# Retention in spans of 64 tokens, two side by side, with a middle state and another order of the steps

## The reference, cut to what matters

```python
def make_decay(length):                       # N_HEADS = 16, HEAD_DIM = 16
    gamma = 1.0 - 2.0 ** (-5.0 - jnp.arange(N_HEADS))
    diff = n - m
    return jnp.where(diff >= 0, gamma ** diff, 0.0)
...
for i in range(2):
    p = layer_norm(x) @ proj_w[i] + proj_b[i]
    q, k, v, xo = jnp.split(p, 4, axis=-1)    # each into 16 heads of 16
    scores = jnp.einsum('bhld,bhmd->bhlm', q, k) * D[None]
    ret = jnp.einsum('bhlm,bhmd->bhld', scores, v)
    ret = ret * jax.nn.silu(xo)
    x = x + ret @ reto_w[i] + reto_b[i]
    h = gelu(layer_norm(x) @ ffn1_w[i] + ffn1_b[i]) @ ffn2_w[i] + ffn2_b[i]
    x = x + h
```

## Time and profile before

| | |
|---|---|
| three runs | 1582.61, 1589.01, 1590.4 us |
| median | 1589.01 us |
| the profiled execution: span from first to last instruction | 1579.5 us |
| the profiled execution: its own time | not given apart from its span |
| TensorE matmul busy | 1351.4 us, 86% of the span |
| DVE busy | 1011.0 us, 64% |
| ACT, POOL busy | 614.6 us, 571.9 us |

### The profile page before, as it was taken

The page is one execution under the profiler, slowest core; times in us unless marked ns, Lnnn a source line. Parts: engine busy times, 40 slices in busy tenths (PEclk is TensorE's granted clock), DMA queues, the critical chain, the costliest instruction groups (busy, mean ns, idle before and its releaser), DMA issues.

```text
span 1579.5 us, 30698 instructions
## 1 busy us (share of the span) xinstructions
PE 1351.4 (86%) x11824; PEld 1104.9 (70%) x11824; DVE 1011.0 (64%) x2391; ACT 614.6 (39%) x1034; POOL 571.9 (36%) x460
## 2 busy tenths in 40 slices
PE   6871968876999999999998999999999676496885
PEld 3461968644788888888886888888887446496753
DVE  5661536658977877777768778797787453253623
ACT  5630635422333433343344334424455262263410
POOL 0726033352342323224424443364343704304252
PEclk9975979989999999999999999999999788698998
DMA  9963559650000000000010000000002463355542
GB/s 326 372 213 122 174 175 321 206 190 23 28 2 2 1 2 1 1 2 32 8 58 1 1 15 2 15 15 14 2 28 89 167 229 131 124 181 171 156 150 90
DMA packets 113867, 151.63 MB, mean 96 GB/s; under 512 B 12224, under 2 KB 96192, under 8 KB 113728
## 3 DMA queue, kind: packets, MB, share of 16 engines
q1 hardware_dynamic: 99328, 114.02, 21.8%
q0 software_dynamic: 12288, 33.57, 6.6%
q10 hardware_dynamic: 2112, 2.10, 0.4%
HBM read 78.21 MB, written 71.43 MB: 95 GB/s over the span
## 4 chain that ended last, share of the span: by engine, by line
PE 53%; DVE 16%; another core or an unknown queue 8%; issue 2%; ACT 2%; POOL 0%; DVEq 0%; ACTq 0%
PE l_w_ps L83 8%; PE l_w_ps L85 7%; PE l_w_ps L84 7%; DVE l_probs L2221 4%; PE l_banks L2505 3%; PE l_rm_ps L2537 2%; PE l_banks L83 2%; PE l_banks L84 2%; PE l_banks L85 2%; DVE l_f_lo L2252 2%; PE l_rm_ps L2530 2%; DVE l_full L2174 1%; PE b_gu_ps L83 1%; PE b_t_ps L1284 1%
## 5 line engine op out<-in xcount | busy, mean ns | idle before, releaser
L2221 DVE TENSOR_TENSOR l_probs<-l_banks,l_past 128x512 f32<-128x512 f32 x256 | 160.1, 684 | 29.8 <-PE l_banks L2505 29.7
L1964 ACT ACTIVATE l_act_f<-l_w_ps,l_ffn_b 128x512 f32<-128x512 f32 x120 | 82.7, 690 | 169.0 <-PE l_w_ps L85 163.9
L83 PE MATMUL l_w_ps<-l_w_hi,l_f_hi 128*128 128x256 f32 x496 | 143.6, 290 | 2.6 <-DVE l_f_lo L2252 2.4
L84 PE MATMUL l_w_ps<-l_w_lo,l_f_hi 128*128 128x256 f32 x496 | 139.6, 281 | 0.0
L85 PE MATMUL l_w_ps<-l_w_hi,l_f_lo 128*128 128x256 f32 x496 | 139.5, 281 | 0.0
L2059 POOL TENSOR_TENSOR l_g_lo<-l_q,l_g_hi 128x1024 fp32r<-128x1024 f32 x16 | 39.1, 2447 | 266.9 <-ACT l_g_hi L1955 266.9
L813 POOL DMA_INDIRECT b_picked<-rows,b_pos_i x64 | 61.1, 955 | 137.4 <-DMA rows<-b_yb 88.5
L83 PE MATMUL l_w_ps<-l_b_hi,l_w_hi 128*128 128x512 f32 x240 | 102.2, 426 | 0.3 <-ACT l_f_hi L1965 0.3
L83 PEld LDWEIGHTS l_w_ps<-l_w_hi,l_f_hi 128*128 128x128 f32 x496 | 93.3, 188 | 8.8 <-issue 8.7
L2252 DVE TENSOR_TENSOR l_f_lo<-l_act_f,l_f_hi 128x512 fp32r<-128x512 f32 x128 | 85.9, 703 | 18.5 <-ACT l_f_hi L1965 18.4
L2046 POOL TENSOR_TENSOR l_q_wide<-l_q,l_pair_mask 128x1024 f32<-128x1024 f32 x32 | 60.1, 1899 | 103.7 <-DVE l_q L2189 100.0
(11 more groups left out here) (432 smaller groups left out, 4053.0 us busy)
## 6 DMA issues: line engine op xcount, KB each, us to landing
rows<-a_zeros SPq DMA_DIRECT2D x14, 1024.0 KB, 10.7
a_xb<-rows SPq DMA_DIRECT2D x46, 256.0 KB
rows<-a_yb SPq DMA_DIRECT2D x46, 256.0 KB
b_xb<-rows SPq DMA_DIRECT2D x46, 256.0 KB
rows<-b_yb SPq DMA_DIRECT2D x46, 256.0 KB
a_w_in<-in_moe_w SPq DMA_DIRECT2D x15, 384.0 KB, 10.2
low_dram<-a_w_lo SPq DMA_DIRECT2D x15, 384.0 KB
b_w_lo<-low_dram SPq DMA_DIRECT2D x15, 384.0 KB
```

The costliest lines, as they stand in the source:

```text
L83: tensor.matmul(out, w_hi, x_hi, start=start, stop=False)
L84: tensor.matmul(out, w_hi, x_lo, start=False, stop=False)
L1964: nc.scalar.activation(act_f[:, f, :], hidden_ps(b, f), ACT.Gelu, bias=ffn1_b[:, b.layer, f:f + 1]).then_inc(act_done, 1)
L2221: dve.tensor_tensor(probs[c % 2][:, r * w:(r + 1) * w].rearrange("p (h n) -> p h n", n=P), banks[:, r, :].rearrange("p (h n) -> p h n", n= ...
```

## The change

- A chunk of 128 tokens is now two spans of 64 (`SPAN`, `SPANS`), done side by side in two halves of the array. Decays, mask and `own_head` are those of 64 tokens.
- `scores`: 16 matmuls instead of 8, on 32 rows by 64 columns, eight tiles, 128 moving columns instead of 256. A bank `banks[:, r]` holds 256 columns of scores instead of 512.
- values (in `retain`): 32 matmuls instead of 16, on 64 rows by 32 columns, eight tiles, 64 moving columns instead of 128.
- `outer`: 16 matmuls instead of 8, on 64 rows by 32 columns, eight tiles, 128 moving columns as before.
- state (in `retain`): 16 matmuls instead of 8, on 128 rows by 32 columns, four tiles, 64 moving columns; the first span takes `state`, the second the new `middle` (the state between the two spans). They now stand behind the values.
- `masked`: 128x256 instead of 128x512, in two pairs with `copy_keys` between them. `update_state`: one product of 128x512 instead of 128x256, then two instructions for `middle` and two for `state`. The last chunk of a batch now has `turn_keys`, `outer` and an update of `middle` too.
- Result, keys and outer products share the two banks of `rm_ps`. So `turn_keys` waits for `gated_done` instead of `state_done`, and `retain` waits until the outer products are read (`state_step`).
- Order on TensorE: scores(c+1), keys, one feed, outer, remaining feeds, values, state. `FEEDS` is now ((0,), (1, 2), (3, 4), (5, 6, 7)).

The core of the diff:

```diff
-        FEEDS = ((0,), (1, 2), (3, 4, 5), (6, 7))
+        FEEDS = ((0,), (1, 2), (3, 4), (5, 6, 7))
...
-        ret_ps, m_ps = rm_ps[:, 0, :], rm_ps[:, 1, :]
+        ret_ps, keys_ps, m_ps = rm_ps[:, :, 0:P], rm_ps[:, :, P:2 * P], rm_ps[:, :, 2 * P:]
...
-                        dve.tensor_tensor(probs[c % 2][:, r * w:(r + 1) * w].rearrange("p (h n) -> p h n", n=P),
-                                          banks[:, r, :].rearrange("p (h n) -> p h n", n=P),
-                                          past[:, :].unsqueeze(1).broadcast_to([P, 4, P]), ALU.mult).then_inc(probs_done, 1)
+                        dve.tensor_tensor(probs[c % 2][:, r * w:(r + 1) * w].rearrange("p (h n) -> p h n", n=SPAN),
+                                          banks[:, r, 0:w].rearrange("p (h n) -> p h n", n=SPAN),
+                                          past[:, 0:SPAN].unsqueeze(1).broadcast_to([P, 4, SPAN]), ALU.mult).then_inc(probs_done, 1)
...
+                        dve.tensor_tensor(fresh[:, 0:n, :, :], products[:, 0:n, :, :], own, ALU.mult).then_inc(state_step, 1)
+                        dve.wait_ge(state_step, before + 1)
+                        for g in range(KD):
+                            last = dve.scalar_tensor_tensor(middle[:, g, :], state[:, (k - 1) % 2, g, :], state_decay[:, g:g + 1],
+                                                            fresh[:, 0, g, :], ALU.mult, ALU.add)
+                        last.then_inc(state_step, 1)
...
+                        for h in range(SPANS):
+                            keys, own = slice(h * SPAN, (h + 1) * SPAN), span(c, h)
+                            for r in range(NQ):
...
+                                last = pe.matmul(banks[keys, r, g * PH * SPAN:(g + 1) * PH * SPAN], kT[rows, g, own], q_wide[rows, g, :, own],
+                                                 start=True, stop=True)
...
+                                last = pe.matmul(m_ps[quad, h, g * P:(g + 1) * P], ks[keys, w],
+                                                 v_wide[keys, c, g * NQ:(g + 1) * NQ, 0::PH, :], start=True, stop=True)
...
+                    pe.wait_ge(state_step, STATE_STEPS * cc - a.batch + (2 if k == 0 else 1))
+                    for g in range(KD):
+                        for i in range(PH):
+                            for h in range(SPANS):
...
+                                    pe.matmul(ret_ps[r * QUAD:(r + 1) * QUAD, h, g * SPAN:(g + 1) * SPAN],
+                                              v_wide[keys, c, g * NQ + r, i:i + PH, :].rearrange("p i x -> p (i x)"),
+                                              probs[c % 2][keys, head * SPAN:(head + 1) * SPAN],
...
+                                w = middle[:, g, quad] if h else state[:, (k - 1) % 2, g, quad]
+                                last = pe.matmul(ret_ps[quad, h, g * SPAN:(g + 1) * SPAN], w, q[:, g, span(c, h)], start=False, stop=(g == KD - 1))
```

More of the change, by code:

```diff
@@ L74 @@
 PH = QUAD // HD
+SPAN = P // 2
+SPANS = P // SPAN
 WEIGHT_PIECES = 2 * KD + 3
@@ new lines, in update_state @@
+                def update_state(a, cc, k):
+                    dve.wait_ge(st_done, cc + 1)
+                    products = m_ps.rearrange("p h (g n) -> p h g n", g=KD)
+                    n = SPANS if k < UPDATES else 1
+                    own = own_head[:, :, :].unsqueeze(1).broadcast_to([P, n, KD, P])
+                    before = STATE_STEPS * cc - a.batch
+                    if k == 0:
+                        dve.tensor_tensor(fresh[:, 1, :, :], products[:, 1, :, :], own_head[:, :, :], ALU.mult).then_inc(state_step, 1)
+                        dve.tensor_tensor(middle[:, :, :], products[:, 0, :, :], own_head[:, :, :], ALU.mult).then_inc(state_step, 1)
+                    else:
+                        dve.tensor_tensor(fresh[:, 0:n, :, :], products[:, 0:n, :, :], own, ALU.mult).then_inc(state_step, 1)
[4 more added lines that the diff above has]
+                        last.then_inc(state_step, 1)
+                    if k == UPDATES:
@@ L2242, in update_state @@
                         return
-                    dve.tensor_tensor(fresh[:, :, :], part, own_head[:, :, :], ALU.mult).then_inc(fresh_done, 1)
-                    dve.wait_ge(fresh_done, (UPDATES - 1) * batch + k)
+                    dve.wait_ge(state_step, before + 2)
                     for g in range(KD):
-                        last = dve.scalar_tensor_tensor(state[:, k % 2, g, :], state[:, (k - 1) % 2, g, :], state_decay[:, g:g + 1],
-                                                        fresh[:, g, :], ALU.mult, ALU.add)
@@ L2248, in update_state @@
-                    last.then_inc(state_done, 1)
+                        last = dve.scalar_tensor_tensor(state[:, k % 2, g, :], middle[:, g, :], state_decay[:, g:g + 1],
+                                                        fresh[:, 1, g, :], ALU.mult, ALU.add)
+                    last.then_inc(state_step, 1)
                 def low_feed(b, f):
@@ L2500, in scores @@
                             pe.wait_ge(k_done, KD * (a.n + 1))
-                        for r in range(NQ):
-                            if g == 0 and c > 0:
-                                pe.wait_ge(probs_done, NQ * (cc - 1) + r + 1)
-                            rows = slice(r * QUAD, (r + 1) * QUAD)
-                            last = pe.matmul(banks[:, r, g * PH * P:(g + 1) * PH * P], kT[rows, g, t], q_wide[rows, g, :, t],
-                                             start=True, stop=True)
-                            if g == KD - 1:
-                                last.then_inc(scores_done, 1)
```

164 lines of the change are left out of this document (86 added, 78 removed).

## The result

The changed kernel is slower. Its median is 1601.7 us (four runs, 1595.96 to 1608.64) against 1585.91 us for the kernel before beside it (four runs, 1582.61 to 1590.4). The ratio is given as 1.0158, 95% interval 1.0117 to 1.020; these two medians alone give 1.0100. So the loss is 16 to 24 us. It lies above my range, and the mechanism that did it is not among my rivals. The profiled execution has a span of 1606.9 us, 27 more than before. It took 1608.6 us, 1.7 more than its span; so the 9.5 us between the span and the median of the kernel before are not time outside the span, as I wrote, but mostly the distance of its profiled run from the median.

What follows compares the result with a forecast made beforehand. TensorE was taken to bound the retention steps. Per step 3.44 us less, minus 1.64, 0.33 and 0.11, nets 1.36; over 16 steps 21.8 us, so 1589.0 becomes 1567 us, range 1553 to 1594.

Steps and rivals of the forecast that it cites:

- two more instructions of 0.31 follow (+0.61): VectorE's state update: two added instructions cost 0.61 us per chunk, beside +0.27 for the wider product.
- So DVE has 0.2 us less per chunk, hidden under PE: VectorE per chunk: masks save 1.08 us, the state update adds 0.27 and 0.61; some 9 us of slack per step.
- Eight tiles side by side: TensorE's scores and values: eight tiles run at once, saving 0.43 us each per chunk, 3.44 us per step.
- rival 1: TensorE runs only four tiles at a time: 1.30 us more per chunk, 1650 us in all; chance 0.11.
- rival 2: A floor of 0.027 us per TensorE matmul: 2.6 us more per chunk, 1733 us in all; chance 0.05.
- Values, 0.43 us of slots: TensorE's 64 values matmuls per chunk: 8 slots of 0.054 us, 0.43 instead of 0.86; bar some 0.65 us.
- Changes of tiling: TensorE switching tile shapes: 0.14 to 0.20 us each, 3.61 us per step instead of 1.97, so 1.64 more.
- Old waits against new ones: TensorE's waits per step: 1.0 us new in chunk 0 against 0.4 to 1.6 gone, set off against each other.
- My 19 us: The gain forecast for the 14 steps behind the first: 19 us shorter.
- my 51.8: Length of a step after the change: about 51.8 us instead of 53.2.
- Fetching of instructions "at nothing": TensorE's list grows by 80 load and matmul pairs in each of 64 chunks; fetching them was costed at nothing.
- If that feed were gone, 1 us per chunk would show: The feed behind the outer products covers VectorE's reading of them before the values; without it, 1 us per chunk.

Runs made afterwards that it cites:

- e1: Changed kernel with GpSimd's two bias additions held back until behind chunk 0's state update: 1577.5 us, 0.9986 of the kernel before.
- e3: Changed kernel with GpSimd's bias additions cut from 256 columns a token group to 4, leaving most of the biases out: 0.9984 of the kernel before.
- e10: Changed kernel with GpSimd's two bias additions put on the state update of chunk 1 in every step: 1.0395 of the kernel before.
- e11: Kernel before the change with GpSimd's two bias additions put on its state update of chunk 1: ratio 1.0012.
- e2: Kernel before the change with GpSimd's two bias additions held back as in e1: 1572.05 us, ratio 0.9966.
- e5: Changed kernel with late additions and, in chunks 1 and 2, half a feed block between two groups of 32 value matmuls: 14 steps take 738.2 us.
- e8: Changed kernel with late additions and, in each step's first feed block, the matmuls that read b_lo issued last: 0.9951 of the kernel before.
- e0: Changed kernel as it is, measured again: 1601.5 us, 1.0150 of the kernel before.
- e7: Kernel before with late additions, and VectorE's second measurement and normalisation of the second tile moved behind the first step's chunk 0: ratio 0.9946.

## Why the prediction was wrong

**The step that failed** is the cost of VectorE's added work: "two more instructions of 0.31 follow (+0.61)", "So DVE has 0.2 us less per chunk, hidden under PE", and "POOL, ACT and the DMA queues get nothing new". I took the price from a chunk 1, where GpSimd is idle. In chunk 0 of each step GpSimd runs its two additions of 2.4 us, and there the two pairs cost up to 4.7 us instead of 1.2. The change gives GpSimd nothing, but it puts twice as many instructions under it. e1 and e3 take the loss away (1.6%), e10 raises it (another 2.4%), e11 shows that the kernel with the shorter chain hardly minds (0.5% over e2). With the additions held back (e1) VectorE is busy for 1002.4 us, 8.6 less than before, so my 0.2 us less per chunk (12.8 in all) was near for a VectorE that GpSimd doesn't hold. The trace of before had the sign. The longest wait of the weight loads for `l_state` in the earlier trace rows is 1.9 us, and its place in the timeline of before shows why:

```profile
845.71 2.40 POOL L2067 TENSOR_TENSOR x_sb<-x_sb,l_bias 128x1024 f32<-128x1024 f32 x1
846.62 1.90 DVE L2246 SCALAR_TENSOR_TENSOR l_state<-l_state,l_state_decay,l_fresh 128x128 f32<-128x128 f32 x2
```

I read that wait as one that would go, and didn't ask what made it long.

**Eight tiles side by side**: right. The 32 score matmuls take 0.69 us (I said some 0.85), the 32 outer products 0.67, so rival 1 is false. By the records, starts of eight lie 6.6 ns apart, so there is no floor of 27 ns, nor of the 25 ns that I quoted, for matmuls on separate tiles, and rival 2 is false in its strong form.

**Values, 0.43 us of slots**: a term mis-sized. The bar is 0.86 us against my 0.65; e5 gives the reason for most of it, 0.14 us a chunk of supply.

**Changes of tiling**: right in price. In e1, from a group's start to the next less its slots, 0.19 us remain for the scores, 0.17 for the outer products and 0.15 for the state.

**Old waits against new ones**: not even. `ks` and `b_lo` cost 0.36 and 0.49 us in chunk 0 and nothing elsewhere in the steps with feeds, some 12 us in all; of the old waits TensorE's 5.5 us for the state went.

**Where e1's gain comes from: luck.** A step has two stretches: its chunks, from `turn_b`'s first matmul to `turn_a`'s, and what lies between the turns. Summed over the 14 steps (us, worked out from the records):

```
                        chunks    between the turns
before                   389.2        353.5
changed                  412.0        339.2
e1 late adds             395.3        339.2
e8 + late low pass       390.5        339.3
e2 before, late adds     385.8        353.5
```

My 19 us were 6 between the turns (the scores of chunk 0, whose group does take 0.44 us less from its start to the next) and 13 in the chunks. In the chunks no form of the changed kernel in this table is faster than before: e1 is 6.1 us slower, e8 1.3. The whole gain lies between the turns, 14.3 us, and 8 of these are a term that I hadn't seen, a wait of `feed_out` for the low feeds. From one turn to the other, every second step took 25.9 us instead of 24.5 (its 96 matmuls 12.83 us instead of 11.48), and it takes 24.1 in each now. A part of it stands in the waits before:

```profile
PE l_w_ps L83 <- DVE l_f_lo L2252: 2.4, 7, 0.3
```

So the step of 52.2 us, near my 51.8, is no proof of my sum. Its chunks take 28.1 us where they took 27.4, and the stretch between the turns 24.1 where it took 25.9.

**Fetching of instructions "at nothing"**: nearly. In e1 TensorE stops within a group with nothing to wait for:

```profile
598.81 0.39 PE L2589 MATMUL l_rm_ps<-l_q,l_middle 128*32 128x64 f32 x10
599.68 0.31 PE L2589 MATMUL l_rm_ps<-l_q,l_middle 128*32 128x64 f32 x6 [0.48 <-issue]
```

It stands behind the 10844th load or matmul of the records, and eight other profiles of the changed kernel stop there too (all but e5's), for 0.20 to 0.77 us. Of the other stops several pairs lie 252 to 256 loads and matmuls apart. A stop that keeps its place in the program, whatever is waited for, points at the fetching of instructions, and the queue of instruction packets grew from 99 to 139 of 16 KB; no run tests it. In e0 four such stops come to 1.9 us in the steps.

**The first step**: not costed at all. I took all 16 steps as equal, but the first has no feeds, and every cover that I named was a feed. "If that feed were gone, 1 us per chunk would show" stands in my text, and it is gone in four chunks. That is 5 to 8 us (e0 33.7 and the changed kernel 35.8, against 28.3).

Of the 19 us forecast for the 14 steps, e1 has 8.2 and e8 13.0, against the kernel before as it was. In the chunks of e1 19 us are missing: the values (7.6) and the new waits less the old (6.5) make 14 of them, and for the rest I have no account beyond the stops. What stays open: the stretch behind the 14 steps varies by some 15 us between profiles of either kernel (436 to 452 us on the chips where the kernel before takes about 1580), and I can't say how much of the loss of 16 to 24 us is there.

## What to carry to other kernels

Price an added VectorE instruction with two SBUF inputs by what GpSimd is doing at that place, not by its mean or by a quiet chunk: sort the group's instances by whether a GpSimd instruction overlaps them. If two such instructions form a chain, each can be held for a whole GpSimd instruction; moving GpSimd's work by one wait cost nothing here. Split the time by stretch before a total that comes near the forecast is taken for its confirmation. And count how many iterations lack the work that covers the others: the first and the last step have an order of their own.

## What the runs showed of the hardware that I had not expected

- The hold is whole and sharp: 349 ns alone, up to 2.4 us beside one addition of 2.4 us, while `bn_stats` and the masks run beside it within 1 ns of their mean alone in the changed kernel.
- Eight tiles accept 32 matmuls in 0.24 us, 7.5 ns each, but 64 take 0.64 us: past some 40 pairs of load and matmul they start more slowly, and with a pause ahead of them they don't.
- TensorE stopped for 0.20 to 0.77 us inside a group of small matmuls, with nothing to wait for, at the same place of the program in nine of ten profiles of the changed kernel.
- Chips differ outside the steps. The 14 steps took 739.3 us in e2 on one chip and 739.1 in e7 on another, but the kernel before took 1579.6 us on the one and 1407.2 on the other. The granted clock, here of e2 and then of e7, is alike in the steps and differs around them:

```profile
PEclk9975988989999999999999999999999878598998
```

```profile
PEclk9989999999999999999999999999999999999999
```
